# Differential attention on one core: ScalarE copies out the turned sums, GpSimd finishes them, VectorE keeps their reciprocals

## The reference, cut to what matters

```python
attn1 = softmax(q1 @ k1.T * scale) @ v     # q1, k1: (b, head, t, 16)
attn2 = softmax(q2 @ k2.T * scale) @ v     # v: (b, head, t, 32)
attn = attn1 - lambda_full * attn2         # 2 x 16 heads of 32 columns
attn = attn * rsqrt(mean(attn * attn) + eps) * norm_w * (1 - LAMBDA_INIT)
out = attn @ wo.T
```

## Time and profile before

| | us |
|---|---|
| median of 3 runs (lowest to highest) | 2482.46 (2478.36 to 2482.72) |
| the profiled execution | 2479.18 |
| its span | 2477.4 |
| TensorE busy in the span | 2344.1 (95%) |
| VectorE busy | 1678.0 (68%) |
| ScalarE busy | 1252.5 (51%) |
| GpSimd busy | 190.1 (8%) |

### The profile page before, as it was taken

How to read it: one execution, slowest core, us unless ns; L and a number is a source line. 1 busy time by engine, 2 the same in 40 slices (tenths; PEclk the granted TensorE clock), 3 DMA queues, 4 the chain that set the end, 5 groups by cost and what they waited for, 6 DMA issues and landing times. The chain is left out here.

```text
span 2477.4 us, 43796 instructions
## 1 busy us (share of the span) xinstructions
PE 2344.1 (95%) x15600; PEld 1331.8 (54%) x15600; DVE 1678.0 (68%) x3848; ACT 1252.5 (51%) x2467; POOL 190.1 (8%) x341
## 2 busy tenths in 40 slices
PE   6999999999999999879999999967999999999877
PEld 5663333333333333458888888856644444444456
DVE  2357888888888887583344434452488888888586
ACT  2126666667666666652221121232266666666653
POOL 3000000000000000100000000000012211221103
PEclk9999999999999999999999999988899999999998
DMA  5664222232122200000000000003622222210001
GB/s 192 165 137 85 57 27 27 33 45 30 27 27 28 27 1 2 31 30 22 26 26 25 25 25 25 1 0 105 142 41 41 41 41 41 40 23 3 27 1 68
DMA packets 56684, 109.09 MB, mean 44 GB/s; under 512 B 11820, under 2 KB 22060, under 8 KB 56488
## 3 DMA queue, kind: packets, MB, share of 16 engines
q1 hardware_dynamic: 53960, 96.84, 19.7%
q0 software_dynamic: 2528, 9.70, 1.1%
HBM read 73.75 MB, written 31.46 MB: 42 GB/s over the span
## 5 line engine op out<-in xcount | busy, mean ns | idle before, releaser
L576 ACT ACTIVATE l_w_hi_prob<-l_p_work 128x512 f32<-128x512 f32 (+3 forms) x1792 | 871.0, 553 | 369.6 <-PE l_p_work L478 351.6
L628 DVE TENSOR_REDUCE l_maxima<-l_p_ring 128x1 f32<-128x512 f32 x1280 | 806.5, 684 | 134.8 <-PE l_p_ring L456 125.5
L498 PE MATMUL l_p_work<-l_w_hi_prob,v_all 128*32 128x512 f32 (+3 forms) x3584 | 806.6, 557 | 1.3 <-POOL l_w_hi_prob L432 0.9
L498 PE MATMUL l_p_work<-l_w_hi_prob,l_ones 128*32 128x512 f32 (+3 forms) x3584 | 806.3, 557 | 0.0
L478 PE MATMUL l_p_work<-xT_all 50*128 50x512 f32 (+3 forms) x1680 | 428.5, 409 | 0.0
L456 PE MATMUL l_p_ring<-xT_all 48*128 48x512 f32 (+3 forms) x1680 | 428.2, 412 | 0.0
L456 PEld LDWEIGHTS l_p_ring<-xT_all 48*128 48x128 f32 x1680 | 216.9, 185 | 233.2 <-DVE l_maxima L628 155.7
L498 PEld LDWEIGHTS l_p_work<-l_w_hi_prob,v_all 128*32 128x32 f32 x3584 | 166.7, 109 | 323.1 <-issue 197.7
L478 PEld LDWEIGHTS l_p_work<-xT_all 50*128 50x128 f32 x1680 | 222.1, 185 | 163.0 <-ACT l_w_hi_prob L576 113.3
L625 DVE CUSTOM_DVE_ANT_0 l_masked_scores<-l_p_ring,l_mask 128x128 bf16<-128x128 f32 (+3 forms) x512 | 239.4, 487 | 54.7 <-PE l_p_ring L456 44.8
L1098 DVE SCALAR_TENSOR_TENSOR ffn_h<-ffn_p_u,ffn_group_scales,ffn_silu 128x512 f32<-128x512 f32 x64 | 48.1, 751 | 211.9 <-PE ffn_p_u L226 205.9
(11 more groups left out here) (148 smaller groups left out, 2921.4 us busy)
## 6 DMA issues: line engine op xcount, KB each, us to landing
xT_all<-q_parts SPq DMA_DIRECT2D x180, 128.0 KB
q_parts<-l_part SPq DMA_DIRECT2D x64, 256.0 KB
xT_all<-k_parts SPq DMA_DIRECT2D x90, 128.0 KB
k_parts<-l_part SPq DMA_DIRECT2D x40, 256.0 KB
xT_all<-k_parts SPq DMA_DIRECT2D x90, 64.0 KB
x<-in_x_T SPq DMA_DIRECT2D x4, 1024.0 KB, 11.3
x<-in_L_attn_x POOLq DMA_DIRECT2D x1, 4096.0 KB, 16.0
out<-x SPq DMA_DIRECT2D x16, 256.0 KB, 2.0
```

Source lines behind the costliest of these rows:

```text
L498: summing = pe.matmul(p_out[r0:r0 + VD, off:CH], lhs, prob[step % PRING][:, sub, off:CH], start=first, stop=final)
L576: act.activation(prob[step % PRING][:, sub, off:CH], p_score[:, at % SCORE_BANKS, off:CH], ACT.Exp, scale=HD ** -0.5).then_inc(exped, 1)
L628: dve.tensor_reduce(to, scores, AX.X, ALU.max).then_inc(freed, 1)
```

## The change

The work of `keep` is split over three engines. VectorE's `invert` makes the reciprocals only. ScalarE's new `copy_turned` waits for the turn and for the reciprocals, and copies the whole bank to a buffer in SBUF (`turned`, one for each chunk, in room that the projections used before); its semaphore `turn_kept` frees the bank. GpSimd's new `keep` multiplies the second softmax's reciprocals by `neg_lambda`, multiplies 256 columns, and adds the halves. `turned_after` puts `copy_turned` behind an exponent, as `copied_after` does for `copy_out`, and GpSimd's `keep` behind the same step. Layer 0's pattern stays as it was. Layer 1 has a new one, and its second chunk's `copy_out` stands one exponent later. The readers of ring banks are counted apart (`read_at`), since two engines free them now. The mask of layer 1 is waited for once at the start, and each product of a pair waits for its own bank.

```diff
+        self.user = {b: x for x, b in self.bank_at.items()}
+        reduced = turned = 0
+        for b in range(bank):
+            if self.user[b][0] == "turn":
+                turned += 1
+                self.read_at[b] = turned
+            else:
+                reduced += 1
+                self.read_at[b] = reduced
...
-           24, (4, 3))
-L1 = Layer("l1", D // 4, D // 4, True, "PVRWSQVTQRVUVRWWWUUQRVQWRURWXQRUQUVWRUQVWUVURQRQWTQVRVUWWWQUV",
-           20, (3, 2))
+           24, (4, 3), (16, 32))
+L1 = Layer("l1", D // 4, D // 4, True, "PRUUWSVRRQQVVWWWQUQPUWQVVUPWXSPRUWTTQSQVQWWWSRRURRSWWV",
+           20, (3, 3), (11, 19))
...
-        recip = sb("recip", [P, QPC, 2, 1], F32)
+            mask, masked = sb("mask", [P, CH], F32), sem("masked")
+        recip = sb("recip", [P, QC, QPC, 2, 1], F32)
+        turned = [part[i][0][:, :].bitcast(F32) for i in range(QC)]
...
+            def keep(n, qc):
+                kept = QC * n + qc
+                cols = turned[qc].rearrange("p (b s w) -> p b s w", b=QPC, s=2)
+                pool.wait_ge(turn_kept, kept + 1)
+                if kept:
+                    pool.wait_ge(out_kept, 3 * kept)
+                pool.tensor_scalar(recip[:, qc, :, 1, :], recip[:, qc, :, 1, :], neg_lambda, None, ALU.mult
+                                   ).then_inc(out_kept, 1)
+                pool.wait_ge(out_kept, 3 * kept + 1)
+                pool.tensor_tensor(half[:, :, :, :], cols[:, :, :, 0:VD],
+                                   recip[:, qc, :, :, :].to_broadcast([P, QPC, 2, VD]), ALU.mult
+                                   ).then_inc(out_kept, 1)
+                tiles = attn[:, :].rearrange("p (t c) -> p t c", c=D)
+                tile = (n // NH) * KT + qc * QPC
+                to = tiles[:, tile:tile + QPC, (n % NH) * VD:(n % NH + 1) * VD]
+                pool.wait_ge(out_kept, 3 * kept + 2)
+                pool.tensor_tensor(to, half[:, :, 0, :], half[:, :, 1, :], ALU.add).then_inc(out_kept, 1)
...
                 for s in range(S):
                     if diagonal(s):
@@ -431,6 +459,14 @@
                         pool.wait_ge(exped, 2 * (n * S + s + 1))
                         pool.affine_select(out=part, in_=part, compare_op=ALU.is_ge, fill=0.0, base=0,
                                            pattern=[[0, 2], [1, P]], channel_multiplier=-1).then_inc(masked, 1)
+                    for m in (n - 1, n):
+                        for qc, last in enumerate(L.qc_last):
+                            if m >= 0 and 2 * (m * S + last) + 1 + L.turned_after[qc] in (2 * (n * S + s) + 1, 2 * (n * S + s)):
+                                keep(m, qc)
+                    if n == HEADS - 1 and s == S - 1:
+                        for qc, last in enumerate(L.qc_last):
+                            if 2 * last + 1 + L.turned_after[qc] > 2 * S - 1:
...
         def _(pe):
             def take_bank(item):
 
-                if L.bank_at[item] >= RING:
-                    pe.wait_ge(freed, L.bank_at[item] - RING + 1)
+                older = L.bank_at[item] - RING
+                if older >= 0 and L.user[older][0] == "turn":
+                    pe.wait_ge(turn_kept, L.read_at[older])
+                elif older >= 0:
+                    pe.wait_ge(freed, L.read_at[older])
...
                 for sub in subs:
-                    take_bank(("maxima", n, u, max(subs)))
+                    take_bank(("maxima", n, u, sub))
...
+            def copy_turned(n, qc):
+                act.wait_ge(filled, L.filled_at["turn", n, qc])
+                if n == 0:
+                    act.wait_ge(stored[qc], 16 * PARTS * len(range(qc, L.units, PART_BUFFERS)))
+                else:
+                    act.wait_ge(out_kept, 3 * (QC * (n - 1) + qc + 1))
+                act.wait_ge(out_recip, QC * n + qc + 1)
+                act.activation(turned[qc], p_ring[:, L.bank_at["turn", n, qc] % RING, :], ACT.Copy
+                               ).then_inc(turn_kept, 1)
...
             for n in range(HEADS):
                 for qc, s in enumerate(L.qc_last):
                     at = 2 * (n * S + s) + 1 + L.copied_after[qc]
-                    copies.setdefault(min(at, 2 * HEADS * S - 1), []).append((n, qc))
+                    copies.setdefault(min(at, 2 * HEADS * S - 1), []).append((copy_out, n, qc))
+            for n in range(HEADS):
+                for qc, s in enumerate(L.qc_last):
+                    at = 2 * (n * S + s) + 1 + L.turned_after[qc]
+                    copies.setdefault(min(at, 2 * HEADS * S - 1), []).append((copy_turned, n, qc))
             for at in range(2 * HEADS * S):
                 exp(*divmod(at // 2, S), at % 2)
...
-            def keep(n, qc):
-                kept, bank = QC * n + qc, L.bank_at["turn", n, qc]
-
+            def invert(n, qc):
+                cols = p_ring[:, L.bank_at["turn", n, qc] % RING, :].rearrange("p (b s w) -> p b s w", b=QPC, s=2)
                 dve.wait_ge(filled, L.filled_at["turn", n, qc])
-                cols = p_ring[:, bank % RING, :].rearrange("p (b s w) -> p b s w", b=QPC, s=2)
-                if kept:
-                    dve.wait_ge(out_kept, kept)
-                dve.reciprocal(recip[:, :, :, 0], cols[:, :, :, VD]).then_inc(out_recip, 1)
-                dve.wait_ge(out_recip, kept + 1)
-                dve.tensor_tensor(half[:, :, :, :], cols[:, :, :, 0:VD], recip[:, :, :, :].to_broadcast([P, QPC, 2, VD]),
-                                  ALU.mult).then_inc(freed, 1)
-                dve.wait_ge(freed, bank + 1)
-                tiles = attn[:, :].rearrange("p (t c) -> p t c", c=D)
-                tile = (n // NH) * KT + qc * QPC
-                to = tiles[:, tile:tile + QPC, (n % NH) * VD:(n % NH + 1) * VD]
-                dve.scalar_tensor_tensor(
-                    out=to, in0=half[:, :, 1, :], scalar=neg_lambda, in1=half[:, :, 0, :],
-                    op0=ALU.mult, op1=ALU.add).then_inc(out_kept, 1)
+                if n:
+                    dve.wait_ge(out_kept, 3 * (QC * (n - 1) + qc + 1))
+                dve.reciprocal(recip[:, qc, :, :, 0], cols[:, :, :, VD]).then_inc(out_recip, 1)
 
             dve.memset(ones[:, :], 1.0).then_inc(ready, 1)
 
             dve.memset(maxima[:, :, :, :], -3e38).then_inc(ready, 1)
-            dve.wait_ge(ready, 3)
+            dve.wait_ge(ready, made)
             for i, (src, to, _) in enumerate(jobs):
```

More of the change, by code:

```diff
@@ L77, with __init__ @@
 class Layer:
-    def __init__(self, name, k_dims, v_dims, causal, pattern, first_pairs, copied_after):
+    def __init__(self, name, k_dims, v_dims, causal, pattern, first_pairs, copied_after, turned_after):
         self.name, self.k_dims, self.v_dims, self.causal = name, k_dims, v_dims, causal
@@ L99, in __init__ @@
         self.qc_last = [max(s for s, x in enumerate(self.steps) if x[0] == qc) for qc in range(QC)]
-        self.pattern, self.first_pairs, self.copied_after = pattern, first_pairs, copied_after
+        self.pattern, self.first_pairs = pattern, first_pairs
+        self.copied_after, self.turned_after = copied_after, turned_after
         self.items = self.projections() + self.heads()
@@ L412, in _ @@
             if L.causal:
-                pool.memset(mask[:, :], 0.0).then_inc(mask_made, 1)
-                pool.wait_ge(mask_made, 1)
+                pool.memset(mask[:, :], 0.0).then_inc(ready, 1)
+                pool.wait_ge(ready, 4)
                 pool.affine_select(out=mask[:, CH - P:CH], in_=mask[:, CH - P:CH], compare_op=ALU.is_ge, fill=MASKED,
-                                   base=0, pattern=[[-1, P]], channel_multiplier=1).then_inc(mask_made, 1)
+                                   base=0, pattern=[[-1, P]], channel_multiplier=1).then_inc(ready, 1)
             if first_load:
@@ L433, in _ @@
                                            pattern=[[0, 2], [1, P]], channel_multiplier=-1).then_inc(masked, 1)
+                    for m in (n - 1, n):
[5 more added lines that the diff above has]
+                            if 2 * last + 1 + L.turned_after[qc] > 2 * S - 1:
+                                keep(n, qc)
                 if n == 1:
@@ L601, in _ @@
                     at = 2 * (n * S + s) + 1 + L.copied_after[qc]
-                    copies.setdefault(min(at, 2 * HEADS * S - 1), []).append((n, qc))
+                    copies.setdefault(min(at, 2 * HEADS * S - 1), []).append((copy_out, n, qc))
[3 more added lines that the diff above has]
+                    copies.setdefault(min(at, 2 * HEADS * S - 1), []).append((copy_turned, n, qc))
             for at in range(2 * HEADS * S):
                 exp(*divmod(at // 2, S), at % 2)
-                for done in copies.get(at, []):
-                    copy_out(*done)
+                for copy, *done in copies.get(at, []):
+                    copy(*done)
         @block.vector
@@ L619, in reduce @@
                     if masking:
-                        if (n, u, sub) == (0, L.masking[0], 0):
```

(7 more changed lines are left out.)

14 lines of the change are left out of this document (6 added, 8 removed).

## The result

| | before | changed |
|---|---|---|
| median, us (lowest to highest, 4 runs each) | 2480.41 (2474.21 to 2482.72) | 2534.72 (2532.86 to 2538.19) |
| ratio of the times, 95% interval | | 1.0226 (1.0207 to 1.0246) |
| span of the profiled execution | 2477.4 | 2531.3 |

A forecast was written before the change was run, and what follows sets the result against it. TensorE's own work was taken to bound both layers, not VectorE. The profiled 2479.2 us plus 23 for layer 1's heads and 5 for the attentions' ends gave 2507, the median put at 2508, with a range from 2473 to 2520.

The forecast's parts named there:

- TensorE alone: Layer 1: without the new wait, one double turn and seven score groups bring a head from 16.61 to 16.32 us.
- What bounds the kernel: Both layers: TensorE's own work is the bound; VectorE, though nearly full, costs layer 0 at most some 0.15 us a head.
- Rival 3: Both layers: VectorE was the bound after all, 1.5 us a head come free, down to some 2440; chance 0.03.
- Layer 0: Layer 0's heads: idle time covers ScalarE's two added copies, some 0.2 us of it left; change 0, heads still 26.2 us.
- Rival 2: Layer 0: ScalarE is late, `copy_out` moves and a sum waits some 0.3 us a head, +9 to 2517; chance 0.09.
- The mechanism in layer 1: Layer 1: step 10's select queues behind two keeps, so TensorE's sum waits 1.05 us a head, +23 us in 30 heads.
- Rival 1: Layer 1: GpSimd is in time, no wait, saving of 0.29 us a head stays: 2474, or 2469; chance 0.22.
- ScalarE's second copy until 0.95: Layer 1's chain: the second copy ends 0.95 us after the start of the group behind the turns, following a reciprocal until 0.33.
- The keeps: GpSimd: a keep takes 1.59 us (0.73 + 0.45 + 0.17 + 3 x 0.08), bounds 1.20 and 1.74.
- The ends: Ends of the attentions: +3.5 us in layer 0 from three keeps in a row, +1.4 in layer 1 from one keep left.
- the last ones have other orders: Layer 1's last heads: set apart as having other orders when the wait was summed over 30 heads to +23 us.

The follow-up runs named there:

- experiment 7: Changed kernel, but ScalarE copies without waiting for the reciprocals and both layer 1 keeps stand behind the next head's step 3: 2489.47 us, a head 16.72.
- experiment 3: Changed kernel with layer 1's new pattern, but VectorE finishes the sums in both layers as before the change: 2491.89 us, a head 16.93.
- 1: Changed kernel, but both keeps of layer 1 stand behind the select of the next head's step 3: 2506.8 us, a head 17.19.
- Experiment 6: Changed kernel, but ScalarE copies without waiting for the reciprocals, which VectorE makes from the copy: 2517.47 us, a head 17.45.
- Experiment 4: Changed kernel's split in both layers, but layer 1 keeps its old pattern, both keeps behind the next head's step 3: 2488.39 us, a head 16.61.
- experiment 5: Split in layer 0 alone; layer 1 has its old pattern and VectorE finishes there: 2482.94 us, ratio 1.0025 to the kernel before.
- experiment 2: Changed kernel, but in layer 1 only the first chunk's keep moves behind the next head's step 3: 2505.35 us, a head 17.19.
- experiment 8: Split with layer 1's old pattern, but the first chunk's keep stands between the selects of step 11 and the next head's step 0: 2507.05 us, a head 17.35.

## Why the prediction was right and wrong

**A head of layer 1, taken apart.** The runs give each layer of the cost:

| kernel | head, us | what it adds |
|---|---|---|
| forecast for TensorE alone | 16.32 | |
| 7, new pattern, both waits gone | 16.72 | +0.11 to before's 16.61 |
| 3, same pattern, VectorE finishes | 16.93 | +0.21 to 16.72, bank held by VectorE's keep |
| 1, split, keeps late | 17.19 | +0.47 to 16.72, bank held until the late copy |
| 6, copy first, keeps in place | 17.45 | +0.73 to 16.72, select late |
| changed kernel | 18.05 | +1.33 to 16.72, both |

**What bounds the kernel: right.** TensorE did, in both layers. Experiment 4 takes 8 us in 100 off VectorE and keeps the heads at 16.61; experiment 5 does the same for layer 0. The total of the weight loads' waits was not a bound, as the text said. Rival 3 is out.

**Layer 0: right.** Heads of 26.21. ScalarE's cover held by little. The idle time ahead of `copy_out` is 0.26 us in the changed kernel, of the 1.06; some 0.2 was foretold:

```profile
496.76 1.08 ACT L614 ACTIVATE l_part<-l_p_ring 128x512 f32<-128x512 f32 x2 [0.51 <-DVE l_recip L706]
497.73 1.58 ACT L625 ACTIVATE l_w_hi_prob<-l_p_work 128x512 f32<-128x512 f32 x3
499.58 0.60 ACT L605 ACTIVATE l_w_hi_sums<-l_p_work 128x512 f32<-128x512 f32 x1 [0.26 <-PE l_p_work L537]
```

Rival 2 did not happen.

**The mechanism in layer 1: right, its size not.** The sum of step 10 waits for a select behind two keeps; with one keep there is no such wait (experiment 2), and in another place there is (experiment 8). Rival 1 is out.

**"TensorE alone 16.32": wrong by 0.40.** This is the first step that failed. Seven groups were priced at 0.26 us plus 0.417 ns a column, a fit to groups of 1408 and 1536 columns. Experiment 7 has 16.72. The two groups of 2048 columns take 1.23 and 1.28 us instead of 1.11, a group of 1408 with products of 128, 256 and 128 columns in its middle 0.91 instead of 0.85, and the one of 1152 columns 0.78 instead of 0.74; the seven sum to 6.79 and not 6.41, which is nearly all of the difference. The price took the fuller half as if it ran without a gap. The trace has gaps. In the long group shown under experiment 7 each half begins with a score of 128 columns, 0.05 us by the price, and the maxima behind it begin 0.16 us later (2083.11 - 2082.95). But the group behind the turns has such a gap too and is only 0.04 too long, so one gap is not all of it; the fuller halves of the long groups have six and five products, that one has four. In the other group of 2048 columns, 0.17 too long, a second cause may have a share: ScalarE's exponents start at 2087.23, one of 128 queries takes 0.28, and the fourth score, which needs that exponent's bank, starts at 2087.56. No run changed the order within a group, so what makes the groups longer is argued and not shown. The saving of 0.29 us from joined turns and fewer groups was more than eaten.

**"ScalarE's second copy until 0.95": wrong by 0.42.** This is the second step. The copies end 1.37 us behind the start of the group (2009.68 + 1.09 - 2009.40). The forecast let the first copy run while the second turn did. But it waits for the first turn's reciprocal, which VectorE does only behind the maxima of 512 that began at 2008.75. That reciprocal starts at 2009.37, so the first copy starts at 2009.68, and the second copy stands behind it. (The second reciprocal, done at 2009.72, holds nothing up.) Had the same question been asked for the first reciprocal as for the select (what is queued ahead of it), this would have been seen. Experiment 6 takes this wait away and gives back 0.60. Everything behind it came as foretold but 0.4 us late: exponent 1.75 for 1.38, select of step 10 5.80 for 5.39, the sum 5.85 for 5.42. One reading of the forecast was off by little: it let ScalarE start an exponent 0.06 us before the last one ends, while two of 0.60 us in 1.08 overlap by 0.12.

**The keeps: right as a sum, by two errors that cancel.** On GpSimd by line and shape, mean ns behind the comma:

```profile
L445 POOL TENSOR_TENSOR l_w_hi_half<-l_part,l_recip 128x256 f32<-128x256 f32 x128 | 78.8, 616 | 10.7
L452 POOL TENSOR_TENSOR attn<-l_w_hi_half 128x128 f32<-128x128 f32 x128 | 58.3, 455 | 10.0
L442 POOL TENSOR_SCALAR l_recip<-l_recip,neg_lambda 128x4 f32<-128x4 f32 x128 | 37.9, 296 | 887.2 <-ACT l_part L614 876.4 <-POOL attn L452 10.8
```

The product of 256 takes 0.616 for 0.73, the product of four columns 0.296 for 0.17, the addition 0.455 for 0.45. Two keeps and the gap between them take 3.22 us (2011.61 to 2014.83) for the 3.10 foretold. The Trainium skill (GPSIMD Engine Reference, Engine selection) puts a two-input operation at about twice VectorE's time; by this trace the shape of L445 takes 616 ns against L659's 425, 1.45 times, with another source of its data.

**The wait for the ring's bank: not in the prediction.** It counted the bank that `copy_turned` frees at nothing. With the keeps out of the way it costs 0.47 us a head (17.19 - 16.72), and here too the late copy is the cause. In the changed kernel it adds nothing to the late select, since TensorE stands still at the sum of step 10 until the same chain is through, whether or not it waited for the bank before: 5.85 - 4.51 = 1.34 us is all that TensorE loses, 4.51 being the time from the group behind the turns to the sum of step 10 without a wait (2084.18 - 2079.67 in experiment 7). So the account closes: 16.72 + 1.34 = 18.06. The forecast's was 16.32 + 5.42 - 4.37 = 17.37. Of the 0.69 us between them 0.40 are TensorE's groups, 0.43 the late copies, and 0.14 are given back, as TensorE reaches the sum later too.

**The ends.** Layer 0's three keeps in a row cost 3.7 us for 3.5 (experiment 5). In layer 1, VectorE's last reciprocal starts 28.0 us behind the last turn of maxima (at 2377.68), where it started 23.4 behind it before (at 2325.07): +4.6. The prediction left this out with "the last ones have other orders". In the last heads the sum of step 10 waits for the select twice more, 3.5 us in all:

```profile
2358.24 0.40 PE L537 MATMUL l_p_work<-l_w_hi_prob,v_all 128*32 128x256 f32 x1 [1.27 <-POOL l_w_hi_prob L460]
...
2375.41 0.40 PE L537 MATMUL l_p_work<-l_w_hi_prob,v_all 128*32 128x256 f32 x1 [2.24 <-POOL l_w_hi_prob L460]
```

What follows takes 2.8 us instead of 1.05, +1.8 for the 1.4 foretold. Of the 5.5 us more ahead of layer 1, these three keeps are 3.7, and 2 lie ahead of the last mark of layer 0 (982.5 before, 984.5 in the changed kernel), 1.0 of them ahead of its first (143.6 and 144.6). They vary from kernel to kernel (last mark at 983.7 in experiment 3, where VectorE finishes), and their cause stays open. 43 + 6 + 5 is the 54 us. Against the forecast, the heads of layer 1 cost 20 us more (43 for 23) and the ends 6 more (11 for 5).

## What to carry to other kernels

When work moves to an idle engine with an in-order queue, its own speed is the small question: list what stands behind it in that queue and who waits for it, and do so for each engine in the chain, down to the instruction of 0.2 us that another engine must do first. Here the same keeps were free behind one select and cost 0.7 to 0.9 us a head ahead of another. And where the bound engine was full, relief of the next one was worth nothing here: only the bound engine's own groups counted, and the price for them did not hold beyond the shapes that it was fitted to.

## What was not expected of the hardware

A per-row multiplication of four columns takes GpSimd 296 ns, half of a product of 256 (616). The second keep starts 0.17 us behind the addition of the first (2013.31 behind 2012.68 + 0.46), twice the 0.08 between the instructions of one keep. The first instruction of a keep stands behind two waits for semaphores and the others behind one; whether that is the cause, no run shows. On TensorE, a group of ten scores and maxima is dearer than the same products in two groups (1.68 against 1.40), with a wait for ScalarE's exponents in it, and one of 2048 columns in its fuller half takes 0.12 to 0.17 us more than the columns and the switch that shorter groups show.
